# Between two graph layers: x1 scaled on ScalarE, first table reads issued among the table's stores, two groups of comparisons placed earlier

## The reference, cut to what matters

```python
h = x @ W1 + b1
m = relu(concat([h[dst], h[src] - h[dst]]) @ W2 + b2)
m = relu(m @ W3 + b3)
x1 = layernorm(x + relu(segment_max(m, dst)))            # 6250 x 128
AX = segment_sum(edge_weight[:, None] * x1[dst], src)    # second layer swaps the roles
out = layernorm(x1 + AX @ WL.T + bL)
```

## Time and profile before

| | |
|---|---|
| median of three runs | 2501.72 us (2500.84 to 2503.64) |
| the profiled execution | 2503.72 us, its span 2501.9 us |
| PE busy in the span | 1942.2 us (78%) |
| DVE, ACT, POOL busy | 1609.3 (64%), 807.9 (32%), 1278.0 us (51%) |
| gathers of `seg_tab` start | 1369.94 us |
| second layer's weight product starts | 1464.08 us |
| first matmul of the second layer's loop | 1487.28 us |

### The profile page before, as it was taken

The page is one execution under the profiler, slowest core; times in us unless marked ns, Lnnn a source line. Parts: engine busy times, 40 slices in busy tenths (PEclk is TensorE's granted clock), DMA queues, the critical chain, the costliest instruction groups (busy, mean ns, idle before and its releaser), DMA issues.

```text
span 2501.9 us, 60027 instructions
## 1 busy us (share of the span) xinstructions
PE 1942.2 (78%) x15568; PEld 1699.8 (68%) x15568; DVE 1609.3 (64%) x4451; ACT 807.9 (32%) x2385; POOL 1278.0 (51%) x1300
## 2 busy tenths in 40 slices
PE   4757678777777778777776359899999997888884
PEld 4646556555565556556554259889888897888884
DVE  3547667767676766767677745445444453888887
ACT  0423233333333333333333125555555554000003
POOL 6246566666666666666663706666666666000000
PEclk7769899999999999998998569999999999999997
DMA  4245455555555555555554227777777776888885
GB/s 120 80 114 154 135 153 151 152 151 151 153 147 151 152 152 149 152 151 152 150 153 109 56 80 237 241 242 242 240 240 244 243 240 220 263 266 267 264 266 169
DMA packets 528061, 447.25 MB, mean 179 GB/s; under 512 B 58459, under 2 KB 493111, under 8 KB 527968
## 3 DMA queue, kind: packets, MB, share of 16 engines
q1 hardware_dynamic: 336516, 208.08, 29.6%
q0 software_dynamic: 53312, 138.17, 17.8%
q10 hardware_dynamic: 138140, 100.06, 13.3%
HBM read 300.43 MB, written 145.64 MB: 178 GB/s over the span
## 4 chain that ended last, share of the span: by engine, by line
PE 47%; issue 14%; another core or an unknown queue 13%; DVE 12%; ACT 4%; DVEq 2%; SPq 2%; DMA 2%; POOL 2%; ACTq 1%; POOLq 0%
PE z_ps L1489 6%; PE t_ps L1489 6%; PE m_ps L1489 6%; PE m_ps L1513 4%; PE z_ps L1415 4%; DVE run L1013 4%; PE z_ps L1513 3%; PE m_ps L1402 3%; PE t_ps L1424 2%; PE t_ps L1513 2%; PE m_ps L1403 2%; DVE whole L991 2%; POOL whole L433 1%; DVEq L1211 1%
## 5 line engine op out<-in xcount | busy, mean ns | idle before, releaser
L426 POOL DMA_INDIRECT whole<-q_tab,src_ti x784 | 763.0, 973 | 485.4 <-remote 237.9
L445 POOL DMA_INDIRECT tab<-whole,row_at x392 | 406.1, 1036 | 281.3 <-issue 83.2
L1143 DVE TENSOR_SCALAR whole<-row_bc,node_id 128x768 f32<-128x768 uint8 x392 | 229.7, 627 | 317.2 <-DMA row_bc<-rel_tab 257.7
L1402 PE MATMUL m_ps<-ident,whole 128*128 128x128 f32 x1568 | 333.7, 292 | 57.3 <-issue 45.0
L654 ACT ACTIVATE m<-m_ps,bias 128x512 f32<-128x512 f32 x196 | 134.7, 687 | 669.7 <-remote 623.0
L1403 PE MATMUL m_ps<-oh,win 128*128 128x128 f32 x1568 | 318.6, 286 | 6.4 <-issue 6.4
L1402 PEld LDWEIGHTS m_ps<-ident,whole 128*128 128x128 f32 x1568 | 262.9, 207 | 79.0 <-issue 76.0
L1200 DVE TENSOR_TENSOR whole<-whole 128x384 f32<-128x384 f32 x440 | 241.6, 550 | 58.9 <-issue 37.9
L1403 PEld LDWEIGHTS m_ps<-oh,win 128*128 128x128 f32 x1568 | 254.0, 203 | 15.6 <-issue 15.5
L940 DVE TENSOR_TENSOR scratch<-s_ps,blk_oh 128x196 f32<-128x196 f32 x196 | 70.6, 360 | 299.6 <-remote 279.3
L1013 DVE TENSOR_TENSOR_SCAN run<-row_bc,run,z_ps 128x512 f32<-128x512 uint8 x195 | 248.2, 1273 | 0.4 <-ACT z_ps L659 0.2
(11 more groups left out here) (281 smaller groups left out, 3509.2 us busy)
## 6 DMA issues: line engine op xcount, KB each, us to landing
win<-p_tab SPq DMA_DIRECT2D x784, 64.0 KB
seg_tab<-run_e ACTq DMA_DIRECT2D x196, 256.0 KB
win<-xw_tab SPq DMA_DIRECT2D x392, 128.0 KB
whole<-tab SPq DMA_DIRECT2D x220, 200.0 KB
whole<-tab ACTq DMA_DIRECT2D x220, 200.0 KB
row_bc<-seg_row_tab SPq DMA_DIRECT2D x196, 128.0 KB
row_bc<-rel_tab SPq DMA_DIRECT2D x196, 96.0 KB
whole<-q_tab,src_ti POOLq DMA_INDIRECT x784
```

Source lines behind the costliest of these rows:

```text
L426: pool.indirect_dma_start(qg[:, g % RING, j, :], None, q_tab[:, :], IOA(ap=src_ti[:, t:t + 1], axis=0)).then_inc(q_ld[g % RING], 16)
L445: pool.indirect_dma_start(tab[:, :], IOA(ap=row_at[0:FR, k:k + 1], axis=0), fat[0:FR, k % RR, :], None).then_inc(fat_st[k // GK % RS], 16)
L1143: last = V.tensor_scalar(pick[:, s, j, :], row_bc[:, s, 0:GK * SLOTS], node_id[:, j:j + 1], None, ALU.is_equal)
L1402: mm(m1_ps[:, s, c], lhsT=qg[:, r % RING, j, :], rhs=ident[:], start=True, stop=False)
```

## The change

Four things, all between the layers; what is computed stays the same.

1. **x1 on ACT.** The 49 scaling instructions move from DVE to ACT, which issues them right after `rstd` of the chunk is there and before it copies the chunk's packed columns.
2. **Reads among the stores.** Each of the first four stores of `xw_tab` counts on a semaphore of its own (`x_ld[b]`, which had counted the loads of x). SP issues six stores, then the windows of group 0, two stores, group 1, two stores, group 2, two stores, group 3, and the last store. Group g waits for store g alone: its windows lie within the first 512 (g + 1) rows. SP's wait for the other nine stores stands behind that, ahead of the row numbers of groups 4 and 5.
3. **Comparisons ahead.** DVE makes `picks` of groups 0 and 1 when all of `x1` is done, and `later_blocks` of both when the packing is done, ahead of its copies of `xw`. For that `pick` moves to where `x1_sums` was and `fat` to where x was, and the clearing of `fat`'s last columns moves behind the weight product.
4. **First write to `tab`.** POOL does not wait for PE's fourth group before the first four writes.

```diff
-        pick = l1(0, UN * CK * GK * SLOTS)...
-        fat = l1(HX * D, RR * RW)...
+        pick = l1(HX * D, UN * CK * GK * SLOTS)...
+        fat = l1(0, RR * RW)...
...
-                if u + 1 < G // 2:
+                if 0 < u and u + 1 < G // 2:
                     pool.wait_ge(fat_ps, 2 * GK * (u + 2))
...
-            for b in range(HX // GT):
-                sp.wait_ge((xw_even, xw_odd)[b % 2], b // 2 + 1)
-                sp.dma_start(xw_tab...).then_inc(xw_st, 16)
...
-            sp.wait_ge(xw_st, 16 * (HX // GT))
+            def xw_store(b):
+                sp.wait_ge((xw_even, xw_odd)[b % 2], b // 2 + 1)
+                sp.dma_start(xw_tab...).then_inc(x_ld[b] if b < UN else xw_st, 16)
+
+            for b in range(UN):
+                xw_store(b)
             for g in range(UN):
+                for b in range(UN + 2 * g, UN + 2 * g + 2):
+                    xw_store(b)
+                sp.wait_ge(x_ld[g], 32)
                 chunks(g)
+            for b in range(3 * UN, HX // GT):
+                xw_store(b)
+            sp.wait_ge(xw_st, 16 * (HX // GT - UN))
...
-            roots(0, 0)
-            for c in range(NC):
+            for c, cols in enumerate(norm_cols):
+                roots(0, c)
+                act.wait_ge(rstd_done, c + 1)
+                for h in range(cols.start, cols.stop):
+                    last = nc.scalar.activation(x1[:, h, :], x1_sums[:, h, :], ACT.Identity, bias=shift_by[:, h:h + 1], scale=rstd[:, h:h + 1])
+                last.then_inc(x1_done, 1)
                 for b in range(NB):
                     if chunk_of[batch(b)[-1]] == c:
                         place(1, b)
-                if c + 1 < NC:
-                    roots(0, c + 1)
...
-                dve.wait_ge(rstd_done, c + 1)
-                for h in range(cols.start, cols.stop):
-                    last = V.tensor_scalar(x1[:, h, :], x1_sums[:, h, :], rstd[:, h:h + 1], shift_by[:, h:h + 1], ALU.mult, ALU.add)
-                last.then_inc(x1_done, 1)
...
+            dve.wait_ge(x1_done, NC)
+            for r in range(2):
+                picks(0, r)
             dve.wait_ge(placed, 2 * H)
             dve.wait_ge(late_ld, 32)
-            V.memset(fat[:, :, SL * KW:], 0.0).then_inc(fat_zero, 1)
+            for r in range(2):
+                later_blocks(0, r)
             for b in range(1, HX // GT, 2):
                 dve.wait_ge(xw_ps, b + 1)
                 V.tensor_copy(xw...).then_inc(xw_odd, 1)
             dve.wait_ge(xw_ps, HX // GT)
-            for r in range(RING):
+            V.memset(fat[:, :, SL * KW:], 0.0).then_inc(fat_zero, 1)
+            for r in range(LATE, RING):
                 step1(0, r)
-                if r < UN:
-                    bias_added(r)
+                if r < LATE + UN:
+                    bias_added(r - LATE)
-            dve.wait_ge(xw_st, 16 * (HX // GT))
+            dve.wait_ge(xw_st, 16 * (HX // GT - UN))
+            for b in range(UN):
+                dve.wait_ge(x_ld[b], 32)
```

## The result

The changed kernel takes 2516.17 us (median of 6 runs, 2511.69 to 2518.35), the kernel before in the same session 2502.65 us (2498.35 to 2506.24): a ratio of 1.0053 with a 95% interval of 1.0039 to 1.0066. It is slower, by 13.5 us, where a gain of 6.1 us was forecast; 2516 lies far outside the range. The profiled execution has a span of 2516.6 us, before it was 2501.9.

What follows compares the result with a forecast made beforehand. The chain of waits between the layers, then PE's second-layer loop, was taken to bound the kernel. Group 4 earlier 8.8, writes - 0.5, x1 - 2.2: 6.1 us gained, 2495.6 from 2501.72; sum's range 2492.5 to 2498.5, overall 2487 to 2501.

Steps and rivals of the forecast that it cites:

- x1 on ACT: Layer norm scalings between the layers: ACT slower than DVE by 1.03, 0.80 and 0.40 us per chunk; a loss of 2.2 us.
- Reads among the stores: Window reads between SP's stores: group 0 starts about 1479.5 instead of 1487.28, group 4 8.8 us earlier, after a 2.1 us pause.
- I count them as covered: First four chunks' 4 x 1.03 = 4.1 us of x1 on ACT, taken as hidden under existing waits of ACT and DVE.
- the stall: DVE's wait of 7.82 us at 1433.86 without a named cause, as POOL's gathers end; taken as cover for x1's first chunks.
- Rival C: The stall is absent in undisturbed executions, so x1 costs between 2.2 and 6.3, middle 4.3: 2497.7 us; chance 0.12.
- The signs that were to tell of a wrong forecast: In the changed profile: weight product starting before 1462, or no pause before group 4.
- what is late next: SP's new wait for nine stores before group 4, with row numbers and windows of groups 4 and 5 queued behind it.
- First write to the table: POOL's four early writes, 0.82 MB beside the last store and group 4's reads: loss between 0 and 3.1 us, taken as 0.5.
- Rival D: Reads and stores slow each other at 199 GB/s: SP 4.1 us later, gain only 2.0, 2499.7 us; chance 0.15.
- Rival E: Second layer's loop: early writes shift POOL's writes against SP's reads for good; at 0.15 us a pair 8.3 slower, 2510; chance 0.08.
- Slower: Outcome class for the whole kernel, made of Rival E and a bit of Rival D: chance 0.09.

Runs made afterwards that it cites:

- e6: e1 with SP's row numbers of groups 4 and 5 ahead of the stores and their windows waiting for stores 4 and 5 alone: 2519.52 us, 0.9950 of the kernel before.
- e8: e1 with POOL's wait ahead of its first four writes put back, undoing the early writes: 2525.45 us, 0.9966 of the kernel before.
- e1: The changed kernel with x1 back on DVE: 2496.82 us against 2504.52 of the kernel before, 0.9980.
- e7: e6 with POOL also waiting for its own gather to land at every eighth gather: 2512.32 us, 0.9923 of the kernel before.
- e12: The kernel of e7 again, in a session without late counts: 0.9970 of the kernel before.
- e16: The kernel of e7 and e12 again, in another session without late counts: 0.9980 of the kernel before.
- e3: The changed kernel, x1 on ACT, with POOL waiting at every fourth gather until it has landed: 0.9981 of the kernel before.
- e4: The kernel before with the same POOL wait at every fourth gather as e3: 1.0004 of the kernel before.
- e5: The changed kernel, x1 still on ACT, with DVE repeating the 49 scalings into a spare buffer: 0.9954 of the kernel before.
- e13: The kernel before, unchanged, profiled in a session without late counts (2215 to 2217 us): 1.0004.
- e10: The kernel of e7 with x1 on ACT, in a session without late counts: 0.9982 of the kernel before.
- e15: The kernel of e10 again, in another session without late counts: 0.9980 of the kernel before.
- e17: The kernel of e7 with POOL also pausing behind each chunk of seven gathers in the first 80 us, without late counts: 1.0022 of the kernel before.
- e18: The kernel of e10 and e15 again, in the session of e17, without late counts: 0.9978 of the kernel before.

## Why the prediction was wrong, step by step

**x1 on ACT** is the step that failed. Its durations were right: ACT's scalings take 3.19, 2.42 and 1.26 us and start 0.73 to 0.77 us after the square root, as forecast. Two things were wrong behind them.
- "I count them as covered" let the first four chunks' 4.1 us vanish in the stall. In sessions without the stall there is no such cover, and the term comes out at 4.0 us, between the forecast's 2.2 and 6.3. Rival C had this (4.3 for x1), for a condition that holds in those sessions.
- The stall was taken for a fixed thing that ends with the gathers and absorbs what lies before it. It is no container: it grows with what the train does. Taking work off DVE removed the gaps, and the waits without an owner grew from 4.3 to 15.0 and 7.7 us on ACT, and with them DVE's longest, then for ACT, from 7.8 to 24.6. The term was mis-sized, 18.1 instead of 2.2, and that is 15.9 of the 19.6 us between the forecast of - 6.1 and the result of + 13.5. The signs that were to tell of a wrong forecast looked the other way (a product before 1462, no pause); it started at 1483.14, and the pause was there.

**Reads among the stores** went as told up to group 0: product to group 0 takes 14.9 us where 15.4 was forecast (1464.1 to 1479.5), without a pause and at 2.92 us a group. For group 4 the sum had 8.8 us of gain and the traces show 7.4. The last store landed 23.9 us behind the product's start instead of 22.1 (1507.04, 3.5 us behind its issue), and the row numbers took 1.58 us instead of 0.93; from there to group 4 it took 5.2 us instead of the 6.2 of before, which hold the same register load (1496.04 to 1497.70 in the trace of before). That is 1.5 us later, and since group 3 ended 0.9 us earlier than forecast, the pause is 4.44 us instead of 2.1. What was missing altogether is the pause's after-effect: behind it group 4 runs in 5.05 us instead of 2.92, at 1.2 GHz, which takes 2.1 us back. The stretches show it (length, busy PE, PEld, DVE, ACT, POOL, then the granted clock, DMA share, GB/s):

```profile
1514.00:1518.00 4.00, 4.00 (x19) 4.00 (x20) 4.00 (x10) 0.88 (x3) 0.00 (x0) 0.50 0.70 198
1519.00:1523.00 4.00, 4.00 (x38) 3.99 (x38) 3.06 (x9) 2.87 (x11) 1.03 (x1) 1.00 0.11 23
```
With that, 5.0 us are left at group 10. Here e6 shows that the wait for nine stores was indeed "what is late next": lifted, it gives 5.9 us.

**First write to the table**: 0.5 us was taken; e8's landmarks differ from e1's by 0.4 and 0.3 us, and their times are from two sessions and can't settle less than some microseconds. **Rival D**, reads and stores in each other's way: the pause under 5 us speaks against it. **Rival E**, a slower rhythm of the loop, has next to no share: group 10 starts 14.1 us later than before (1534.07 against 1520.01) and the execution ends 14.7 later, so 0.6 us are lost in all that follows.

**The range and the chances.** The sum's own range was given as 2492.5 to 2498.5, which is 3 us to either side; the bounds named for it (2.2 to 4 for x1, 0 to 3.1 for the writes) give 2495.1 to 2500.0. Slower had 0.09, nearly all of it on E. The mechanism that came true, a train of gathers that delays counts, was in no rival, though the profile had several long waits without an owner, all beside gathers.

## What to carry to other kernels

An owner-less wait is no free cover: before putting work under it, ask what makes it, and whether the change touches that. An engine that is not on the critical path can be too smooth: where GpSimd issues indirect gathers back to back, a short wait every four or eight of them is worth trying, and taking work off an engine beside it can be a loss. And measure in more than one session, on more than one chip: the same change was 1.0053 in one and 0.9997 in another, while "read a window behind its own store" (e6, and a part of e7) shortened product to group 10 in either, from 50.6 to 44.7 us and from 50.5 to between 44.6 and 46.9.

The best version is e7: 0.9923 (0.9906 to 0.9939) in a session with late counts, 0.9970 and 0.9980 without. e6, without pauses, should be the better one there; it was not run in such a session, and by the landmarks it would gain what e12 and e16 gain plus the 4.2 us of the pauses, an estimate of about 0.4 to 0.5%.

## What the runs showed of the hardware

- Counts from PE to ACT arrived 13 and 20 us late while 31 indirect gathers ran at 0.94 us each with 0.30 us between them, and one that DVE posted for itself 7.8 us late (before). With a wait of some 1.9 us at every fourth gather (e3, e4) the stage has no wait for such a count, with one at every eighth (e7) one of 2.5 us. Gathers of 2.05 to 2.82 us among them (before, e1, e5) lessen them only: waits of up to 12.8 us were left in e1, on PE, part of which it would have idled anyway.
- This differs by session. In the first loop ACT waited 623.0 us, 179 times, without a named owner in one (before), and 462.0 us, 196 times, for PE in the other (e13); the same program takes 2502 and 2217 us, and its trace holds 25786 and 64157 records of counts.
- PE ran group 4 in 5.05 to 5.46 us behind a pause of 4.0 to 4.6 us (granted clock 0.50 in the changed kernel and e8), in 4.54 behind 1.85 to 1.99 (e10, e12, e15; 0.61 in e10), and in 2.92 behind 1.47 to 1.83 (e6, e16, e17, e18; 1.00 in e6, e16 and e17).
